# A graph layer's inner node stages: row sums in the add, squares on ScalarE, two tiles ahead

## The chip, the cores and the metric

The kernel runs on one core of one Trainium2 chip. The metric is the device time of one execution in microseconds; a median over several runs is given, lower is better. Five engines work side by side, each through a queue of its own: TensorE (PE in the profile, its weight loads PEld), VectorE (DVE), ScalarE (ACT), GpSimd (POOL) and Sync (SP), which here only issues transfers. They meet through semaphores that the program writes out by hand.

## The reference, cut to what matters

`x` has 6250 rows of 256. Three graph attention layers run over 200,000 edges, beside an attention mixer and, at the end, eight experts. Between two graph layers each node's row is put together, normalised and projected for the next layer:

```python
def _layernorm(x, g, b):
    mu = x.mean(-1, keepdims=True)
    var = ((x - mu) ** 2).mean(-1, keepdims=True)
    return (x - mu) / jnp.sqrt(var + LN_EPS) * g + b
...
h = x
for i, (W, a_s, a_d, b, g, be, heads, concat) in enumerate(layers):
    h_new = _layernorm(_gat_conv(h, src, dst, W, a_s, a_d, b, heads, concat), g, be)
    if i > 0:
        h_new = h_new + h
    h = jax.nn.relu(h_new)
```

Inside `_gat_conv` a node's result is the sum over its incoming edges, one of which is the node itself, each weighted by a softmax. The kernel adds the node's own edge in the stage that follows the edges.

## The kernel before, in words

The program is a row of phases with a barrier after each: `prepare_walk`, then `node_phase` of layer 0, then for each layer `edge_phase` and, after the first two, `node_phase` of the next layer; then `final_phase` and `experts`. The change is in `node_phase` (L568) and in `over_ring` (L454), which unrolls its loops. Layer 0 is called `first` in the code and does less; the two others (layers 1 and 2) are the inner node stages.

A node stage goes over NB = 49 tiles of 128 rows. Tiles live in rings of four buffers (`TILE_RING`), so buffer `slot` serves tiles slot, slot + 4 and so on. `over_ring` writes out the first four or eight tiles, loops over groups of four, and ends with tile 48. `acc`, with the edges' sums of all 49 tiles, stays in SBUF. Each engine has its own stream of steps:

- Sync (L656 to L686): loads own rows (`rows`, L648) and in layer 2 the residual's old rows (`prev`, L650) into the ring, both on one semaphore per buffer. For each tile b in turn it waits until h of tile b is ready, stores it (L662), issues the loads for tile b + 4, and stores the projected rows of tile b - 2 (L669) when they are ready.
- GpSimd (L709, L704): for each tile, the sums in `acc` times their share of the softmax (`weigh_sum`), then the own rows times theirs into the ring `O` (`weigh_own`). The second waits for the loaded rows and for h of tile b - 4, which frees the buffer. Both count on `owned`.
- VectorE (L748 to L812): `gather_in` waits for the rows and both products, adds them (L760), and takes mean and variance with the statistics operation (L763) and its aggregate (L766). `finish` waits for ScalarE's square root, takes its reciprocal (L776), scales (L786) and shifts (L790) and in layer 2 adds the residual (L799); the last one counts on `h_ready`. A step runs the `gather_in` of the next tile interleaved with the `finish` of this one, operation by operation. Operations of one tile that depend on each other wait for the one ahead by semaphore.
- ScalarE (L851 to L890): a step for tile b takes the root for tile b + 1 (L853), copies tile b's transpose out of PSUM (L867, with the relu), then for tile b - 1 copies the projection's parts out (L878, L879, L880) and clears that tile of `acc` by copying zeros over it (L883).
- TensorE (L904, L913, L914): transposes h of tile b, then projects tile b - 1: four matmuls in two row halves and one for the bias.

Ahead of the tiles VectorE computes all softmax shares at once and ScalarE takes one exponential; then GpSimd may begin.

Of the kernel before, what the change touches and what calls it, by code (L numbers as in the profile page):

```python
# [17 lines left out]
ALU = mybir.AluOpType  # L18
# [435 lines left out]
def over_ring(eng, step, peeled=1):  # L454

    assert NB % TILE_RING == 1
    for i in range(peeled):
        for slot in range(TILE_RING):
            step(i, slot, False)
    with eng.Fori(peeled, NB // TILE_RING) as i:  # L460
        for slot in range(TILE_RING):
            step(i, slot, False)
    step(NB // TILE_RING, 0, True)

# [8 lines left out]
def padded_ring_rows(dram, i, slot):  # L473
    return dram[bass.ds((TILE_RING * i + slot) * P, P), :]
# [93 lines left out]
def node_phase(nc, layer, st, io, dr):  # L568
# [6 lines left out]
    first = layer == 0  # L575
    acc, AD, own, terms = st["acc"], st["AD"], st["own"], st["terms"]
    with Phase(nc, f"node{layer}") as ph:
# [6 lines left out]
        stats = ph.sb("stats", [P, TILE_RING, 6])  # L584
# [7 lines left out]
        zeros = ph.sb("zeros", [P, GW])  # L592
# [14 lines left out]
        loaded = [ph.sem(f"loaded{k}") for k in range(TILE_RING)]  # L607
        chain1 = ph.sem("chain1")
# [26 lines left out]
        loads = 1 + (layer >= 2)  # L635
# [9 lines left out]
        def _(sp):  # L645
            def load(i, slot, last):
                if not first:
                    sp.dma_start(rows[:, slot, :], padded_ring_rows(dr["rows"], i, slot)).then_inc(loaded[slot], 16)  # L648
                if layer >= 2:
                    sp.dma_start(prev[:, slot, :], padded_ring_rows(dr["h"], i, slot)).then_inc(loaded[slot], 16)  # L650

            load(0, 0, False)
            load(0, 1, False)
            if not first:
                for n, name in enumerate(("ln_g", "ln_b")):
                    sp.dma_start(vecs[:, n, :], broadcast_row(io[f"{name}{layer - 1}"])).then_inc(vecs_in, 16)  # L656
            for slot in (2, 3):
                load(0, slot, False)
# [12 lines left out]
            for b in range(NB):  # L671
                store_h(b)
                if b + TILE_RING < NB:
                    load((b + TILE_RING) // TILE_RING, b % TILE_RING, b + TILE_RING == NB - 1)
                if b >= 2:
                    store_rows(b - 2)
            for b in (NB - 2, NB - 1):
                store_rows(b)
            for slot in range(TILE_RING):
                n = NB // TILE_RING + (slot == 0)  # L680
                sp.wait_ge(h_out[slot], 16 * n)
                sp.wait_ge(ext_out[slot], 16 * n)
                if first:
                    sp.wait_ge(hT_out[slot], 16 * n)

        @block.gpsimd  # L686
        def _(g):
            g.memset(eps[:, :], LN_EPS).then_inc(consts, 1)
            g.memset(ones3[:, :], 1.0).then_inc(consts, 1)
            if not first:  # L690
                g.memset(zeros[:, :], 0.0).then_inc(consts, 1)
# [6 lines left out]
            def weigh_own(b):  # L698
                slot = b % TILE_RING
                g.wait_ge(loaded[slot], 16 * loads * (b // TILE_RING + 1))  # L700
                if b >= TILE_RING:

                    g.wait_ge(h_ready, b - TILE_RING + 2)
                g.tensor_tensor(by_head(O[:, slot, :]), head_view(rows[:, slot, :]),  # L704
                                es[:, 0, b, :].unsqueeze(2).broadcast_to([P, H, D]), ALU.mult).then_inc(owned, 1)
# [12 lines left out]
        def _(v):  # L718
# [26 lines left out]
            N1 = 1 if first else 2  # L745
            N2 = 1 if first else 2 + (layer >= 2)

            def gather_in(i, slot, last):  # L748

                b = TILE_RING * i + slot  # L750
                ch = Chain(v, chain1, b * N1)
                if first:
                    o = acc[:, bass.ds(b, 1), 0:C].rearrange("p a c -> p (a c)")
                else:
                    v.wait_ge(loaded[slot], 16 * loads * (i + 1))
# [4 lines left out]
                    ch.add(v.tensor_tensor(oh, oh, a, ALU.add))  # L760
                    yield
                    ch.wait()
                ch.add(v.bn_stats(stats[:, slot, :], o))  # L763
                yield
                wait_apart(v, chain1, ch.base + ch.n, passed)
                v.bn_aggr(mv[:, slot, :], stats[:, slot, :]).then_inc(stats_ready, 1)  # L766
                assert ch.n == N1

            def finish(i, slot, last):
# [15 lines left out]
                else:  # L785
# [8 lines left out]
                    else:  # L794
# [3 lines left out]

                        v.scalar_tensor_tensor(out=hn, in0=prev[:, slot, :], scalar=0.0, in1=o, op0=ALU.max, op1=ALU.add  # L799
# [3 lines left out]
            for _ in gather_in(0, 0, False):  # L803
                pass

            def step(i, slot, last):

                following = iter(()) if last else gather_in(i + (slot + 1) // TILE_RING, (slot + 1) % TILE_RING, False)
                for _ in zip_longest(following, finish(i, slot, last)):
                    pass  # L810

            over_ring(v, step)  # L812
# [17 lines left out]
        def _(a):  # L830
# [20 lines left out]
            def std(slot, b):  # L851
                a.wait_ge(stats_ready, b + 1)
                a.activation(sd[:, slot, :], mv[:, slot, 1:2], ACT.Sqrt, bias=eps[:, :]).then_inc(sd_ready, 1)  # L853

            std(0, 0)

            def step(i, slot, last):

                b = TILE_RING * i + slot
                if not last:  # L860
                    std((slot + 1) % TILE_RING, b + 1)
# [10 lines left out]
            def extend(i, slot):  # L872
# [8 lines left out]
                if not first:  # L881

                    a.activation(acc[:, bass.ds(b, 1), :].rearrange("p a c -> p (a c)"), zeros[:, :], ACT.Copy).then_inc(acc_clear, 1)  # L883

            over_ring(a, step, peeled=2)
# [4 lines left out]
            if not first:  # L890
                a.wait_ge(acc_clear, NB)
# [1922 lines left out]
```

## Time and profile before

| | |
|---|---|
| median of 3 runs | 7522.47 us (7515.94 to 7524.8) |
| profiled execution, its own time | 7531.31 us |
| its span in the profile | 7529.6 us |
| VectorE busy | 5498.7 us, 73% |
| TensorE busy | 5390.2 us, 72%, mean granted clock 0.779 |
| GpSimd busy | 5176.0 us, 69% |
| ScalarE busy | 2138.7 us, 28% |
| transfers | 949.93 MB, mean 126 GB/s |

The shares are of the whole span, most of which are the three edge phases; for a stage one has to look at its own stretch. The two inner node stages lie at about 2301 to 2432 us and 4557 to 4712 us. Busy time counts an instruction from its start to its end, also while it waits inside for a port or for its predecessor. The granted clock is a share of TensorE's 2.4 GHz. "Waits" lists put an engine's idle time down to what ended it.

### The profile page before, as it was taken

How to read it: one execution, taken by the hardware profiler on the slowest of the kernel's cores; microseconds unless marked ns; L12 is line 12 of the kernel's file. 1: busy time of each engine (PE TensorE's matmuls, PEld its weight loads, DVE VectorE, ACT ScalarE, POOL GpSimd, SP SyncE). 2: the span in 40 equal slices, each digit the busy share in tenths (PEclk: the TensorE clock that was granted, in tenths of full speed). 3: DMA queues.
4: the chain of work that ended last, by engine and by line, in shares of the span. 5: the costliest groups of instructions: out<-in, count | busy, mean ns of one | idle time of the engine just before them, and what ended most of it. 6: DMA issues, size and time to landing. Idle time of an engine off the chain costs nothing. (4 is left out here: it accounts for less than half of the span.)

```text
span 7529.6 us, 113108 instructions
## 1 busy us (share of the span) xinstructions
PE 5390.2 (72%) x23828; PEld 3495.0 (46%) x23829; DVE 5498.7 (73%) x16160; ACT 2138.7 (28%) x5415; POOL 5176.0 (69%) x5471
## 2 busy tenths in 40 slices
PE   5677777766775677777766666587777876673399
PEld 3344444444443345444544444355555544342398
DVE  6677777777777677777777778677787777778643
ACT  2112121211113233333321113234343421113466
POOL 1777777777774777777777773777777777772444
PEclk8777787877778777777777777678888877776599
DMA  6445455544443444444444444444444444444444
GB/s 211 138 141 145 141 146 141 144 135 140 136 134 116 117 121 123 121 123 122 122 114 111 111 110 139 115 123 128 126 128 125 127 118 111 111 111 139 146 70 64
DMA packets 531615, 949.93 MB, mean 126 GB/s; under 512 B 117850, under 2 KB 366049, under 8 KB 531030
## 3 DMA queue, kind: packets, MB, share of 16 engines
q0 software_dynamic: 259808, 691.84, 34.5%
q1 hardware_dynamic: 254610, 235.89, 10.2%
q10 hardware_dynamic: 16612, 15.96, 0.6%
q8 instruction: 177, 2.90, 0.2%
q14 instruction: 408, 3.34, 0.1%
HBM read 796.92 MB, written 151.73 MB: 126 GB/s over the span
## 5 line engine op out<-in xcount | busy, mean ns | idle before, releaser
L1250 POOL DMA_INDIRECT edges_G<-rows,edges_index x4980 | 4749.4, 954 | 1554.4 <-issue 1481.0
L1450 PE MATMUL edges_ps_o<-edges_G,edges_OH 128*128 128x264 f32 x9960 | 3507.1, 490 | 307.1 <-DVE edges_G L1726 173.9
L1450 PEld LDWEIGHTS edges_ps_o<-edges_G,edges_OH 128*128 128x128 f32 x9960 | 2119.1, 234 | 1127.4 <-issue 634.9
L1744 DVE TENSOR_TENSOR acc<-acc,edges_ps_o 128x264 f32 x2490 | 1048.8, 421 | 821.7 <-PE edges_ps_o L1450 547.6
L1726 DVE TENSOR_TENSOR edges_G<-edges_G,edges_ps_c 128x1024 f32<-128x1024 f32 x1245 | 1500.3, 1205 | 1.8 <-ACT edges_G L1270 1.3
L1294 ACT ACTIVATE edges_OHT<-edges_ps_far 128x512 bf16<-128x512 f32 x1245 | 742.5, 596 | 1331.2 <-PE edges_ps_far L1410 1330.8
L1418 PE MATMUL edges_ps_s<-ident,edges_alpha 128*128 128x128 f32 x249 | 114.4, 459 | 1266.5 <-DVE edges_alpha L1620 1266.5
L1718 DVE TENSOR_TENSOR edges_OH<-edges_ps_c,relT 128x512 f32<-128x512 f32 x1245 | 848.6, 682 | 0.1
L1602 DVE COPY edges_node<-terms 128x12 bf16 x2490 | 476.1, 198 | 292.1 <-issue 73.8
L1418 PEld LDWEIGHTS edges_ps_s<-ident,edges_alpha 128*128 128x128 f32 x249 | 44.2, 177 | 1375.3 <-DVE edges_alpha L1620 1375.3
L1410 PE MATMUL edges_ps_far<-edges_rels,pole_rows 5*128 5x512 bf16 x1245 | 608.4, 489 | 41.3 <-DMA WT<-in_L_mix_b 19.8
L1269 ACT ACTIVATE edges_ps_c<-edges_diff 128x80 f32<-128x80 f32 x249 | 60.0, 241 | 1467.6 <-DVE edges_diff L1706 1467.5
L1410 PEld LDWEIGHTS edges_ps_far<-edges_rels,pole_rows 5*128 5x128 bf16 x1245 | 117.2, 94 | 685.3 <-issue 511.5
L1615 DVE TENSOR_TENSOR edges_tu<-edges_ad,edges_G 128x80 f32<-128x80 f32 x249 | 75.0, 301 | 427.9 <-DMA edges_G<-rows,edges_index 427.0
L2581 POOL DMA_INDIRECT out<-experts_Y,experts_token x105 | 165.2, 1573 | 249.7 <-DMA out<-experts_Y,experts_token 210.6
L1293 ACT ACTIVATE edges_front<-edges_ps_far 128x1 f32<-128x1 f32 x249 | 42.7, 171 | 848.7 <-PE edges_ps_far L1410 848.7
L1280 ACT ACTIVATE edges_fade<-edges_ps_s,edges_front 128x4 f32<-128x4 f32 x249 | 65.7, 264 | 758.7 <-PE edges_ps_s L1437 758.7
L2158 POOL DMA_INDIRECT xslot<-final_XH,final_slots x98 | 101.5, 1036 | 167.7 <-DVE final_slots L2338 139.7
L2607 PEld LDWEIGHTS experts_psH<-experts_xs,experts_Wup 128*128 128x128 f32 x1680 | 206.1, 194 | 5.3
L2607 PE MATMUL experts_psH<-experts_xs,experts_Wup 128*128 128x128 f32 x1680 | 206.4, 277 | 0.0
L2616 PE MATMUL experts_psY<-W,experts_hT 128*128 x840 | 198.6, 379 | 0.2 <-ACT experts_hT L2666 0.2
L913 PE MATMUL node_psB<-Wx,node_hT 128*128 128x264 f32 x588 | 185.4, 445 | 0.0
(377 smaller groups left out, 6211.3 us busy)
## 6 DMA issues: line engine op xcount, KB each, us to landing
edges_G<-rows,edges_index POOLq DMA_INDIRECT x4980
xslot<-edges_blank SPq DMA_DIRECT2D x80, 650.0 KB
edges_masks<-lanes_of SPq DMA_DIRECT2D x123, 192.0 KB
rows<-node_ext SPq DMA_DIRECT2D x147, 130.0 KB, 2.2
experts_X<-xslot SPq DMA_DIRECT2D x105, 130.0 KB, 2.1
node_rows<-rows SPq DMA_DIRECT2D x98, 130.0 KB
h<-node_Hn SPq DMA_DIRECT2D x98, 128.0 KB, 1.7
W<-in_L_ffn_W SPq DMA_DIRECT2D x16, 512.0 KB
```

What stands on the lines that cost most here:

```text
L913: pe.matmul(psB[slot % 2][:, 0:RW + H], hT[:, slot % TILE_RING, k, :], Wx[:, k, :], start=(k == 0), stop=False)
L1250: g.indirect_dma_start(G[n][:, s, 0:RW], None, dr["rows"], bass.IndirectOffsetOnAxis(index[n][:, s:s + 1], 0)).then_inc(gathered[n], 16)
L1294: a.activation(OHT[:, 4 * k:4 * k + 4, :].rearrange("p s e -> p (s e)"), ps_far[:, :], ACT.Relu, bias=1.0, scale=-1.0).then_inc(oht_ready, 1)
L1410: pe.matmul(ps_far[:, :], pole[r, :], rels[r, 4 * k * P:4 * (k + 1) * P], start=True, stop=True).then_inc(far_ready, 1)
L1450: mm = pe.matmul(ps_o[BANK_OF[g]][:, 0:GW], OH[:, 2 * g + j, :], G[n][:, 2 * g + j, :], start=(j == 0), stop=(j == 1))
L1602: ins = v.tensor_copy(node[n][:, g, :], terms[:, bass.ds(b, 1), :, :].rearrange("p a h k -> p (a h k)"))
L1718: v.tensor_tensor(OH[:, 4 * k:4 * k + 4, :], ps_iota.unsqueeze(1).broadcast_to([P, 4, P]), rel.unsqueeze(2).broadcast_to([P, 4, P]), ALU.i ...
L1726: v.tensor_tensor(g4[:, :, :, 0:D], g4[:, :, :, 0:D], ps_w[:, 4 * k:4 * k + 4, :].unsqueeze(3).broadcast_to([P, 4, H, D]), ALU.mult).then_ ...
L1744: v.tensor_tensor(a, a, ps_o[BANK_OF[g]][:, 0:GW], ALU.add).then_inc(added, 1)
L2581: g.indirect_dma_start(out, bass.IndirectOffsetOnAxis(token[:, slot, :], 0), Y[:, slot, :], None, bounds_check=N - 1, oob_is_err=False, co ...
L2607: mm = pe.matmul(psH[slot % 2][:, c * P:(c + 1) * P], Wup[:, slot % 2, k, c * P:(c + 1) * P], xs[:, slot % 2, k, :], start=(k == 0), stop= ...
L2616: mm = pe.matmul(psY[slot % 2][:, 0:C], hT[:, slot % 2, c * P:(c + 1) * P], W2[:, bass.ds(e, 1), c, :].rearrange("p a o -> p (a o)"), star ...
```

## The change

In the two inner node stages:

- VectorE's add becomes a scalar-tensor-tensor operation (times 1.0, plus) that also writes the row's sum into `total`; the statistics operation and its aggregate go. It is issued two tiles ahead instead of one, and at the start of a step, not interleaved.
- ScalarE turns the sum into the mean, squares the centred row with the operation's own summing (into the variance's place), waits for both, and takes the root with the scale that belongs to it. It does so two tiles ahead.
- ScalarE no longer clears `acc`. Sync does, with a transfer from a fourfold zero tile for four tiles at a time, once their rows are summed.
- Sync loads own rows for tile b + 6 as soon as the products of tile b + 2 are done, ahead of the result's store; the residual's old rows have a semaphore of their own, and only the operation that adds them waits for it.
- `over_ring` takes a number of groups to write out at its end, so that the last step's look-ahead can be left out.

The diff, cut to its core:

```diff
-def over_ring(eng, step, peeled=1):
+def over_ring(eng, step, peeled=1, behind=0):
...
-    with eng.Fori(peeled, NB // TILE_RING) as i:
+    with eng.Fori(peeled, NB // TILE_RING - behind) as i:
+        for slot in range(TILE_RING):
+            step(i, slot, False)
+    for i in range(NB // TILE_RING - behind, NB // TILE_RING):
         for slot in range(TILE_RING):
             step(i, slot, False)
     step(NB // TILE_RING, 0, True)
+
+def within(i, slot, ahead):
+    return not isinstance(i, int) or TILE_RING * i + slot + ahead < NB
...
+    LOOK = 1 if first else 2
...
+            def clear(b, n):
+                sp.wait_ge(stats_ready, b + n)
+                sp.dma_start(acc[:, b:b + n, :], zeros[:, 0:n, :]).then_inc(acc_clear, 16)
...
-            for slot in (2, 3):
-                load(0, slot, False)
+                for b in (2, 3):
+                    load_rows(b)
+                if layer >= 2:
+                    for b in range(TILE_RING):
+                        load_prev(b)
+                for b in range(2):
+                    sp.wait_ge(owned, 2 * b + 2)
+                    load_rows(b + TILE_RING)
+                sp.wait_ge(consts, 3)
...
             for b in range(NB):
                 store_h(b)
-                if b + TILE_RING < NB:
-                    load((b + TILE_RING) // TILE_RING, b % TILE_RING, b + TILE_RING == NB - 1)
+                if not first and b + TILE_RING + 2 < NB:
+                    sp.wait_ge(owned, 2 * (b + 2) + 2)
+                    load_rows(b + TILE_RING + 2)
+                if layer >= 2 and b + TILE_RING < NB:
+                    load_prev(b + TILE_RING)
                 if b >= 2:
                     store_rows(b - 2)
+                if not first and b % TILE_RING == 1:
+                    clear(b - 1, TILE_RING)
+            if not first:
+                clear(NB - 1, 1)
             for b in (NB - 2, NB - 1):
                 store_rows(b)
+            if not first:
+                sp.wait_ge(acc_clear, 16 * (NB // TILE_RING + 1))
...
-                g.memset(zeros[:, :], 0.0).then_inc(consts, 1)
+                g.memset(zeros[:, :, :], 0.0).then_inc(consts, 1)
...
-                    v.wait_ge(loaded[slot], 16 * loads * (i + 1))
...
-                    ch.add(v.tensor_tensor(oh, oh, a, ALU.add))
-                    yield
-                    ch.wait()
-                ch.add(v.bn_stats(stats[:, slot, :], o))
+                    v.scalar_tensor_tensor(out=oh, in0=oh, scalar=1.0, in1=a, op0=ALU.mult, op1=ALU.add,
+                                           accum_out=total[:, slot, :]).then_inc(stats_ready, 1)
+                    return
...
+                        v.wait_ge(prev_in[slot], 16 * (i + 1))
                         v.scalar_tensor_tensor(out=hn, in0=prev[:, slot, :], scalar=0.0, in1=o, op0=ALU.max, op1=ALU.add
...
-                following = iter(()) if last else gather_in(i + (slot + 1) // TILE_RING, (slot + 1) % TILE_RING, False)
-                for _ in zip_longest(following, finish(i, slot, last)):
+                ahead = gather_in(i + (slot + LOOK) // TILE_RING, (slot + LOOK) % TILE_RING, False)
+                for _ in zip_longest(ahead if within(i, slot, LOOK) else iter(()), finish(i, slot, last)):
...
+                a.activation(mv[:, slot, 0:1], total[:, slot, :], ACT.Identity, scale=1.0 / C).then_inc(squared, 1)
+                a.activation(square[:, :], O[:, slot, :], ACT.Square, bias=total[:, slot, :], scale=-float(C),
+                             accum_out=mv[:, slot, 1:2]).then_inc(squared, 1)
+                a.wait_ge(squared, 2 * b + 2)
+                a.activation(sd[:, slot, :], mv[:, slot, 1:2], ACT.Sqrt, bias=eps[:, :], scale=1.0 / C ** 3).then_inc(sd_ready, 1)
...
-                if not last:
-                    std((slot + 1) % TILE_RING, b + 1)
+                if within(i, slot, LOOK):
+                    std((slot + LOOK) % TILE_RING, b + LOOK)
...
-                    a.activation(acc[:, bass.ds(b, 1), :].rearrange("p a c -> p (a c)"), zeros[:, :], ACT.Copy).then_inc(acc_clear, 1)
```

## Rows read from the trace of the kernel before

**Rows 1.** List by tile, node_Hn: count, duration ns min/median/max, first and last start
```profile
L790 DVE SCALAR_TENSOR_TENSOR node_Hn<-node_O,node_rstd,node_vecs x49: 483/485/719, 2312.6 to 2426.1; 128x256 f32<-128x256 f32 x49
L799 DVE SCALAR_TENSOR_TENSOR node_Hn<-node_prev,node_O x49: 424/424/803, 4568.7 to 4705.7; 128x256 f32<-128x256 f32 x49
```

**Rows 2.** Table by stretch: PE, PEld, DVE, ACT, POOL us (count), clock, DMA, GB/s
```profile
2313.00:2427.00 114.00, 80.51 (x334) 49.11 (x335) 97.85 (x286) 65.20 (x284) 60.14 (x92) 0.92 0.52 162
4569.00:4706.00 137.00, 104.52 (x330) 62.93 (x330) 114.75 (x334) 64.46 (x279) 60.59 (x91) 0.70 0.57 178
```

**Rows 3.** List of waits, first inner stage: us in total, times, longest us
```profile
POOL node_O L704 <- DMA node_rows<-rows: 48.6, 44, 2.8
...
ACT AD L878 <- PE node_psB L914: 42.9, 49, 1.9
...
DVE node_rstd L776 <- ACT node_sd L853: 13.3, 30, 1.7
...
DVE node_O L760 <- POOL node_O L704: 1.5, 1, 1.5
```

**Rows 4.** List by tile, node_O, columns as in rows 1
```profile
L704 POOL TENSOR_TENSOR node_O<-node_rows,node_es x98: 607/614/884, 2309.0 to 4698.8; 128x256 f32<-128x256 f32 x98
L760 DVE TENSOR_TENSOR node_O<-node_O,acc x98: 410/420/872, 2309.7 to 4701.6; 128x256 f32<-128x256 f32 x98
L763 DVE BATCH_NORM_STATS2 node_stats<-node_O x98: 408/427/430, 2310.5 to 4702.1; 128x6 f32<-128x256 f32 x98
L786 DVE SCALAR_TENSOR_TENSOR node_O<-node_O,node_mv,node_vecs x98: 467/470/907, 2312.1 to 4704.6; 128x256 f32<-128x256 f32 x98
```

**Rows 5.** Order of time, first inner stage, VectorE and GpSimd: start us, us, instruction
```profile
2340.97 0.47 DVE L786 SCALAR_TENSOR_TENSOR node_O<-node_O,node_mv,node_vecs 128x256 f32<-128x256 f32 x1
2341.03 0.88 POOL L709 TENSOR_TENSOR acc<-acc,node_es 128x256 f32<-128x256 f32 x1
...
2341.48 0.72 DVE L790 SCALAR_TENSOR_TENSOR node_Hn<-node_O,node_rstd,node_vecs 128x256 f32<-128x256 f32 x1
...
2343.18 0.91 DVE L786 SCALAR_TENSOR_TENSOR node_O<-node_O,node_mv,node_vecs 128x256 f32<-128x256 f32 x1
2343.19 0.61 POOL L709 TENSOR_TENSOR acc<-acc,node_es 128x256 f32<-128x256 f32 x1
```

**Rows 6.** Order of time near that stage's end, VectorE, no product beside it
```profile
2422.08 0.48 DVE L790 SCALAR_TENSOR_TENSOR node_Hn<-node_O,node_rstd,node_vecs 128x256 f32<-128x256 f32 x1
...
2422.48 0.42 DVE L760 TENSOR_TENSOR node_O<-node_O,acc 128x256 f32<-128x256 f32 x1
...
2425.36 0.17 DVE L776 RECIPROCAL node_rstd<-node_sd 128x1 f32<-128x1 f32 x1 [0.63 <-ACT node_sd L853]
2425.57 0.48 DVE L786 SCALAR_TENSOR_TENSOR node_O<-node_O,node_mv,node_vecs 128x256 f32<-128x256 f32 x1
...
2426.09 0.48 DVE L790 SCALAR_TENSOR_TENSOR node_Hn<-node_O,node_rstd,node_vecs 128x256 f32<-128x256 f32 x1
```

**Rows 7.** Groups of instructions by form, first inner stage, ScalarE: busy us, mean ns
```profile
L867 ACT ACTIVATE node_hT<-node_psA 128x256 f32<-128x256 f32 x49 | 18.8, 384 | 6.4 <-PE node_psA L904 5.4
...
L853 ACT ACTIVATE node_sd<-node_mv,node_eps 128x1 f32<-128x1 f32 x49 | 14.5, 295 | 6.8 <-DVE node_mv L766 6.8
...
L878 ACT ACTIVATE AD<-node_psB 128x4 f32 x40 | 6.9, 174 | 34.4 <-PE node_psB L914 34.4
...
L883 ACT ACTIVATE acc<-node_zeros 128x264 f32 x40 | 17.0, 425 | 0.0
...
L853 ACT ACT_TABLE_LOAD x1 | 1.3, 1283 | 0.0
```

**Rows 8.** List by line, L2425 of a later stage, ScalarE, columns as in rows 1
```profile
L2425 ACT ACTIVATE final_XH<-final_Hn,final_shift,final_scale x49: 583/585/599, 6867.9 to 7076.5; 128x256 f32<-128x256 f32 x49
```

**Rows 9.** List by tile, node_rows and node_prev, Sync's issues, columns as in rows 1
```profile
L648 SPq DMA_DIRECT2D node_rows<-rows x98: 319/433/461, 2301.6 to 4696.1; - x98
...
L650 SPq DMA_DIRECT2D node_prev<-h x49: 422/457/570, 4557.3 to 4696.6; - x49
```

## What the change will do: the prediction, made blind

> **What bounds the kernel now.** Only the two inner node stages change, so I looked for their stretches first and asked what each tile costs there. The list by tile gives the starts of the operation that finishes a tile: 49 of them from 2312.6 to 2426.1 us in the first inner stage and from 4568.7 to 4705.7 us in the second [rows 1]. Divided by 48 that is 2.364 and 2.854 us per tile, 250 us of 7529.6 in all; nothing else in the program can change much.
>
> Then the table by stretch [rows 2]: VectorE is busy 97.85 of 114 us and 114.75 of 137; the next, TensorE, 80.51 and 104.52; GpSimd and ScalarE about half. The list of waits [rows 3] says the rest: VectorE waits 13.3 us for ScalarE's square root in the first stage and only 1.5 us, once, for GpSimd, although GpSimd itself waits 48.6 us for its own rows to land. So late rows cost nothing yet; VectorE's queue sets the pace.
>
> Last, why VectorE's operations take what they take [rows 4]: those with two tensor inputs reach from 410 to 872 and from 467 to 907 ns, while the statistics (one input) stay within 408 to 430. The order of time shows the reason [rows 5]. The scaling that began at 2343.18, 0.01 us ahead of a GpSimd product, ended 0.29 us after that product. A product that began 0.06 us after a scaling (2341.03 against 2340.97) ended 0.47 us after it, and the next VectorE operation 0.29 us after the product. So the two engines take turns, for 0.29 us of each VectorE operation and 0.47 us of each product; the first 0.12 to 0.19 us of a VectorE operation and 0.14 of a product (0.61 - 0.47) lie beside anything.
>
> **The change, part by part.** *VectorE* loses the statistics (0.427 us) and the aggregate behind them in both stages, and the add becomes one that also sums. No row has such an operation. Nearest is the scaling, also two tensors: 0.470 against 0.420 for the plain add [rows 4]. Bounds: 0.42, and 0.93 (twice the streaming, 0.29 more, and a readout as long as the 0.17 us small reciprocal [rows 6]). I take 0.47, the nearest row.
>
> The Trainium skill, Vector Engine (DVE) Microarchitecture Reference, section 7, says that the scalar-tensor-tensor form with two non-bf16 SBUF sources runs at half throughput, for want of a port to read the accumulator back. The scaling is of that form with two fp32 sources and is not half as fast; no row has the accumulating form, which is the rule's case. By the rule the sum is that of the second rival below.
>
> The new chain, undisturbed spacings from [rows 6]: reciprocal to scaling 0.21, scaling to shift 0.52 (each waits for the one ahead), shift to the next tile's first operation 0.40, that is 0.08 ahead of the shift's end. Laid out with the turns, 0 being the end of a tile's last operation: the sum starts at -0.08, takes its turn 0.10 to 0.39. Weighing the own rows of a later tile, which waits for just that end to get its buffer, takes the next turn, 0.39 to 0.86. Reciprocal at 0.31, scaling at 0.52; it wants its turn at 0.71, gets 0.86 to 1.15. The other product waits until then: 1.15 to 1.62. Shift at 1.19, turn 1.62 to 1.91. So **1.91 us a tile** in the first stage. In the second the residual add follows 0.04 us later, 0.42 long [rows 1], with GpSimd waiting for its end: **2.37**. Without a collision it would be 1.52 and 1.98.
>
> *ScalarE* loses the clear (0.425) and gains a small scaling, a square of 256 with a sum, and a wait for both ahead of the root. Bounds from [rows 7]: the small one 0.174 to 0.295; the square between the clear's 0.425 (264 wide) and 0.585 (256 wide, with two per-partition operands [rows 8]), I take 0.50, as it has one; the readout of the sum nothing to 0.295, I take 0.17. With root 0.295, the two wide copies 0.384 each and the two narrow 0.174 each: 2.26, less five joints where operations overlap by about 0.1 (the clear's 0.425 spans more than its place), plus 0.04 for the wait: **1.80** (1.55 to 2.13). Under 1.91, but close. Its waits for the projection (42.9 us, 0.88 a tile [rows 3]) then cover root work. Will the root be late? Behind the end of tile b-1 come TensorE's 1.67 us (below) and 0.55 of narrow and wide copies, some 0.3 after the end of b; squares and root take 1.0; VectorE wants root b+2 at 1.91 + 0.3: 0.9 to spare. So the 13.3 us wait goes; next in line to be late is ScalarE's whole turn (rival 1).
>
> *TensorE* needs 80.51/114 x 2.364 = 1.67 us a tile at granted clock 0.92 (mostly the 2.4 GHz level) and 104.52/137 x 2.854 = 2.18 at 0.70 (a mixture with the 1.2 GHz level) [rows 2]. If the first stage runs some 9 of its tiles as the second ran, 2.18 instead of 1.91, that costs 2.4 us, which I take (bounds nothing and 13 us, for all 48); in the second it stays under the pace.
>
> *Sync's queue* (every issue counts): at most some 0.46 us an issue [rows 9]; three and a quarter a tile are 1.5, four and a quarter 1.95, under the pace. Its new wait for weighed rows b+2 has behind it that load, the result's store and the clear; VectorE needs those rows before it can end tile b, so it passes at once; so does the wait for the sums. Rows for tile b+6 leave at most 0.9 us after the end of b and are wanted two tiles later, 3.8 us; should they come late, GpSimd slips, and VectorE has one more tile of lead. Cost nothing; without that cover each late row costs its lateness.
>
> *Transfers*: busy share 0.52 x 2.364 = 1.23 us a tile for three, 1.63 for four [rows 2], so 0.41 each. A clear of 132 KB per tile at that price: 1.64 of 1.91 and 2.04 of 2.37, 86%. Nothing, as long as it stays under 1. GpSimd's fourfold zeros (0.9 us more) lie in its wait ahead of the shares. The last clear is issued ahead of the last two stores, so it ends nothing.
>
> *Ends*: one tile more is summed and squared before the first is finished, about 1 us a stage.
>
> **Sum**: (2.364 - 1.91) x 48 = 21.8; (2.854 - 2.37) x 48 = 23.2; less 2.4, less 2: 40.6 us. Against the profiled execution, 7531.3, that is 7490.7; that execution lies 8.8 us above the median of the runs, 7522.5, so the median goes to **7482**.
>
> **Rivals.**
> 1. *ScalarE becomes the bound.* For: 1.80 against 1.91, and two of its operations have no row. At its upper prices 2.13: gain (2.364 - 2.13) x 48 + 23.2 - 4.4 = 30, 7492. If a quarter of its 0.88 us wait is uncovered as well, 2.35: almost only the second stage gains, 19.5, 7503. Against: all its other operations overlap today.
> 2. *The summing add takes the upper price, 0.93.* Same layout: turn to 0.68, product to 1.15, scaling to 1.46, product to 1.93, shift to 2.22; 2.68 in the second stage. Gain 6.9 + 8.4 - 4.4 = 11, 7511, which is no change that can be told. Against: the scaling at 0.470.
> 3. *Slower: the turns are held for whole operations.* Then a tile costs the sum of VectorE's two-input operations and both products: 0.47 + 0.47 + 0.485 + 2 x 0.614 = 2.65, 3.08 with the residual. That is (0.29 + 0.22) x 48 = 24 us more than now, 7547. It decides in the first stage once held time exceeds 2.364. For: the products now find no one-input operation to lie beside. Against: today's sum, 0.42 + 0.47 + 0.485 + 1.23 = 2.60, already exceeds the 2.364 that a tile takes. The Trainium skill, SBUF — State Buffer, Who interferes with whom, states this rule: an exclusive lock for the whole instruction, the loser fully blocked. The trace agrees that one waits for the other, and disagrees on the length.
> 4. *The change doesn't do what it says*: square and root don't share ScalarE's loaded table, and each tile loads twice. A load is 1.283 us [rows 7]; 1.80 + 2.57 = 4.37 a tile, (2.01 + 1.52) x 48 = 169 us more, 7691. For: no row has a square. Against: today's copies and root run behind one load per stage. The Trainium skill, ScalarE: Activation LUTs, Table sets, puts cheap functions into every set and doesn't list square among its examples.
>
> **Chances.** Forecast 0.63 (its own range 7463 to 7500; below lies the layout without collisions but ScalarE-bound, some 65 us), ScalarE 0.17, dear sum 0.11, whole-operation turns 0.05, tables 0.04. A measurement here can tell 0.2%, 15 us, so 7507. Faster: 0.63 + 0.15 + 0.02 = 0.80; same 0.02 + 0.08 = 0.10; slower 0.10. The range 7463 to 7512 holds the forecast nearly whole, the first rival and half of the second: 0.8.
>
> **What would show it.** Starts of the finishing operation 1.9 and 2.4 us apart; VectorE's summing add near 0.47 without a collision, products near 0.8 for having to wait; no wait for the root; one table load a stage; transfers' share near 0.85. Spacing of 2.1 or more with VectorE waiting for ScalarE means rival 1; a summing add above 0.7, rival 2; VectorE operations that end 0.4 us and more behind a product, rival 3. The prediction is wrong in its base if transfers land so late that VectorE waits for GpSimd.

## The result and the profile after

The change makes the kernel faster: 7475.84 us (median of 4, 7471.14 to 7477.6) against 7521.8 (median of 4, 7515.94 to 7524.8), ratio 0.9938, 95% interval 0.9922 to 0.9954, 46 us. Forecast were 7482 and a range of 7463 to 7512. The profiled execution took 7475.3 us, its span is 7473.6.

The list by tile of the changed kernel, the lines that answer to [rows 1]:

```profile
L819 DVE SCALAR_TENSOR_TENSOR node_Hn<-node_O,node_rstd,node_vecs x49: 483/717/927, 2309.0 to 2400.9; 128x256 f32<-128x256 f32 x49
L829 DVE SCALAR_TENSOR_TENSOR node_Hn<-node_prev,node_O x49: 424/425/718, 4540.2 to 4652.0; 128x256 f32<-128x256 f32 x49
```

(2400.9 - 2309.0) / 48 is 1.915 us a tile, (4652.0 - 4540.2) / 48 is 2.329. Times 48 the two stages gain 21.6 and 25.2 us, 46.8 together; the layout had 1.91 and 2.37, 45.0. From the first load of rows to the first finished tile the first stage takes 12.2 us instead of 11.0, the forecast microsecond for one more tile summed ahead. (The two profiled spans differ by 56 us; some 9 of it lie outside these stages, as the profiled execution of before was that far above its median.)

The table by stretch, columns as in [rows 2]:

```profile
2309.50:2400.90 91.40, 75.18 (x328) 46.02 (x329) 82.98 (x236) 77.65 (x371) 63.40 (x89) 0.95 0.85 266
4540.70:4652.00 111.30, 80.54 (x330) 49.36 (x330) 102.46 (x284) 78.79 (x370) 65.01 (x89) 0.91 0.91 273
```

The share of the transfers is 0.85 and 0.91 (0.52 and 0.57 before), TensorE's granted clock 0.95 and 0.91: in the second stage it now runs mostly at the 2.4 GHz level, where it was a mixture before (0.70). The order of time of one tile, VectorE and GpSimd:

```profile
2352.57 0.72 DVE L819 SCALAR_TENSOR_TENSOR node_Hn<-node_O,node_rstd,node_vecs 128x256 f32<-128x256 f32 x1
...
2353.20 0.41 DVE L790 SCALAR_TENSOR_TENSOR node_O<-node_O,acc 128x256 f32<-128x256 f32 x1
...
2353.43 0.67 POOL L737 TENSOR_TENSOR node_O<-node_rows,node_es 128x256 f32<-128x256 f32 x1 [0.42 <-DVE node_Hn L819]
...
2353.55 0.08 DVE L790 DVE_READ_ACCUMULATOR node_O<-node_O,acc 128x1 f32 x1
2353.55 0.15 DVE L805 RECIPROCAL node_rstd<-node_sd 128x1 f32<-128x1 f32 x1
...
2353.74 0.63 DVE L815 SCALAR_TENSOR_TENSOR node_O<-node_O,node_mv,node_vecs 128x256 f32<-128x256 f32 x1
...
2354.05 0.79 POOL L742 TENSOR_TENSOR acc<-acc,node_es 128x256 f32<-128x256 f32 x1
...
2354.41 0.72 DVE L819 SCALAR_TENSOR_TENSOR node_Hn<-node_O,node_rstd,node_vecs 128x256 f32<-128x256 f32 x1
...
2355.15 0.42 DVE L790 SCALAR_TENSOR_TENSOR node_O<-node_O,acc 128x256 f32<-128x256 f32 x1
```

This is the order of the forecast layout. About the end of the last shift (2353.29) the sum runs first, the product of own rows waits and ends at 2354.10, the scaling 0.27 after it, the second product waits for the scaling, 0.79 instead of 0.61, and the shift waits for that product, 0.72 instead of 0.48. From shift to shift this tile takes 1.84 us (2354.41 - 2352.57), and that is the steady tile: 24 of the first stage's 48 spacings are 1.83 to 1.90. In the second stage 30 of 48 are 2.29 to 2.31, while every fourth is about 2.62, where VectorE's loop over groups of four starts anew (why was not looked into). Three finishing operations there:

```profile
4611.65 0.43 DVE L829 SCALAR_TENSOR_TENSOR node_Hn<-node_prev,node_O 128x256 f32<-128x256 f32 x1
...
4613.95 0.43 DVE L829 SCALAR_TENSOR_TENSOR node_Hn<-node_prev,node_O 128x256 f32<-128x256 f32 x1
...
4616.57 0.43 DVE L829 SCALAR_TENSOR_TENSOR node_Hn<-node_prev,node_O 128x256 f32<-128x256 f32 x1
```

The layout's 1.91 and 2.37 are therefore 0.07 above the tile that they describe, and meet the means of 1.915 and 2.329 only because longer tiles, for which the layout has no term, are averaged in. The list by tile, answering to [rows 4], and the list of waits in the first stage, answering to [rows 3]:

```profile
L737 POOL TENSOR_TENSOR node_O<-node_rows,node_es x98: 607/663/907, 2304.1 to 4645.4; 128x256 f32<-128x256 f32 x98
L790 DVE SCALAR_TENSOR_TENSOR node_O<-node_O,acc x98: 410/418/829, 2304.9 to 4647.2; 128x256 f32<-128x256 f32 x98
L790 DVE DVE_READ_ACCUMULATOR node_O<-node_O,acc x98: 75/81/84, 2305.5 to 4647.6; 128x1 f32 x98
L889 ACT ACTIVATE node_square<-node_O,node_total x98: 491/507/526, 2305.7 to 4649.4; 128x256 f32<-128x256 f32 x98
L889 ACT ACTIVATION_READ_ACCUMULATOR node_square<-node_O,node_total x98: 185/198/218, 2306.1 to 4649.8; 128x1 f32 x98
L815 DVE SCALAR_TENSOR_TENSOR node_O<-node_O,node_mv,node_vecs x98: 483/633/859, 2308.4 to 4650.9; 128x256 f32<-128x256 f32 x98
```

```profile
POOL node_O L737 <- DVE node_Hn L819: 13.7, 28, 1.2
POOL node_O L737 <- DMA node_rows<-rows: 9.8, 15, 1.9
...
DVE node_rstd L805 <- ACT node_sd L892: 2.1, 4, 0.8
...
DVE node_O L790 <- POOL node_O L737: 0.6, 1, 0.6
```

The summing add has a median of 418 ns and a readout of 81 ns as an instruction of its own; the square is 507 and its readout 198. The wait for the root is 2.1 us where it was 13.3, and GpSimd now waits for freed buffers more than for rows.

### The profile page after: what moved, and what is told of

It reads as the page before. It is cut to its first block and busy times, and to the rows that moved or that the text cites. A ratio compares the mean times of both kernels' runs of the same rounds, so it can differ in the third digit from the quotient of the medians.

```text
span 7473.6 us, 113007 instructions
## 1 busy us (share of the span) xinstructions
PE 5382.7 (72%) x23828; PEld 3486.5 (47%) x23829; DVE 5479.1 (73%) x16062; ACT 2166.4 (29%) x5611; POOL 5173.5 (69%) x5471
## 5 line engine op out<-in xcount | busy, mean ns | idle before, releaser
L1435 PEld LDWEIGHTS edges_ps_s<-edges_node,edges_OHT 128*128 128x128 bf16 x4980 | 161.3, 96 | 45.3 <-ACT edges_OHT L1329 7.2
```

Source lines behind the costliest of these rows:

```text
L1435: mm = pe.matmul(ps_ad[:, s * KEPT:(s + 1) * KEPT], OHT[:, s, :], node[n][:, s // 2, :], start=True, stop=True)
```

## The experiments

The first account was the prediction's: VectorE's chain, shortened by the statistics, and its turns with GpSimd set the pace. Rivals: the transfers set it; the distance is the gain and the sums aren't. Each row has the spacing per tile in both stages, worked out as above from the one profiled execution, and the ratio to the kernel before. "Sums" names the engine that takes mean and variance, "ahead" the tiles of look-ahead; "early" means that the load for tile b + 6 stands behind the store of tile b in Sync's queue, where the load for b + 4 stood ("late"). The residual's own semaphore is in all rows but the first.

| kernel | sums | ahead | rows | clear | 1st | 2nd | ratio (95%) |
|---|---|---|---|---|---|---|---|
| before | VectorE | 1 | late | ScalarE | 2.364 | 2.854 | 1 |
| after | ScalarE | 2 | early | transfer | 1.915 | 2.329 | 0.9938 (0.9922 to 0.9954) |
| e1_clear_scalar | ScalarE | 2 | early | ScalarE | 1.896 | 2.327 | 0.9937 (0.9921 to 0.9954) |
| e2_one_ahead | ScalarE | 1 | early | transfer | 2.477 | 2.819 | 1.0011 (1.0002 to 1.0021) |
| e3_late_rows | ScalarE | 2 | late | transfer | 2.794 | 3.065 | 1.0044 (1.0027 to 1.0061) |
| e4_statistics | VectorE | 2 | early | transfer | 1.904 | 2.410 | 0.9945 (0.9928 to 0.9961) |
| e7_sums_alone | ScalarE | 1 | late | ScalarE | 2.881 | 3.379 | 1.0053 (1.0038 to 1.0069) |
| e8_ahead_and_rows | VectorE | 2 | early | ScalarE | 1.902 | 2.415 | 0.9944 (0.9931 to 0.9958) |
| e10_rows_alone | VectorE | 1 | early | ScalarE | 2.290 | 2.802 | 0.9990 (0.9981 to 0.9999) |
| e11_ahead_alone | VectorE | 2 | late | ScalarE | 2.842 | 3.100 | 1.0055 (1.0040 to 1.0071) |

**One part undone at a time.** First the clear, back on ScalarE:

```diff
+                if not first:
+                    a.activation(acc[:, bass.ds(b, 1), :].rearrange("p a c -> p (a c)"), zeros[:, 0, :], ACT.Copy).then_inc(acc_clear, 1)
...
-                if not first and b % TILE_RING == 1:
-                    clear(b - 1, TILE_RING)
```

> The changed kernel, but the clearing of acc goes back from transfers to ScalarE. Theory (VectorE's chain and its turns with GpSimd set the pace, 1.915 and 2.329 us a tile; ScalarE stands behind it at about 1.76): ScalarE rises by 0.31 to about 2.07, so the first inner stage goes to about 2.07 and the second stays near 2.33; some 7 us more than the changed kernel, about 7483. Rival (the transfers, busy for 0.86 and 0.90 of the stages, set the pace): the share falls by a quarter and both stages get shorter, under 1.9 and 2.3, or stay.

Its table by stretch, first and second inner stage:

```profile
2307.00:2397.50 90.50, 82.70 (x328) 46.26 (x329) 82.20 (x236) 85.98 (x416) 64.11 (x89) 0.97 0.66 200
4536.50:4647.70 111.20, 83.06 (x330) 50.53 (x330) 101.90 (x283) 91.52 (x416) 64.68 (x89) 0.89 0.71 215
```

The theory's 2.07 did not come, nor the rival's shorter stages. The transfers' share fell to 0.66 and 0.71 and the pace stayed, so in the changed kernel transfers don't set it; and ScalarE had room for the clear: busy 85.98 / 90.5 x 1.896 = 1.80 us a tile with it, 1.63 without. Moving the clear was worth nothing.

Then the distance, one tile instead of two:

```diff
-    LOOK = 1 if first else 2
+    LOOK = 1
```

> The changed kernel with sums and roots one tile ahead instead of two. Theory: ScalarE takes root b+1 only after the copies of tile b-2 (some 2.4 us after the end of tile b-1), 1.0 more for mean, squares and root, and then VectorE needs 1.25 to 1.6 to the end of tile b+1; so two tiles take 4.7 to 5.0, 2.35 to 2.5 a tile in the first stage and about 0.25 more in the second, with VectorE waiting for ScalarE's root: 7515 to 7525, the gain gone. Rival (VectorE's shorter queue is the gain, the distance is of no account): 1.9 and 2.35 as before, 7476.

In its list of waits of the first stage:

```profile
DVE node_rstd L805 <- ACT node_sd L892: 37.1, 46, 2.1
```

As the theory had it (2.477; the second stage a little above): VectorE waits 37.1 us for the root, as ScalarE has the squares to do ahead of it (with the statistics on VectorE the wait is 13.8, e10 below), and the whole gain is gone.

Then the rows, loaded after the tile's end as before:

```diff
-                for b in range(2):
-                    sp.wait_ge(owned, 2 * b + 2)
-                    load_rows(b + TILE_RING)
...
-                if not first and b + TILE_RING + 2 < NB:
-                    sp.wait_ge(owned, 2 * (b + 2) + 2)
-                    load_rows(b + TILE_RING + 2)
+                if not first and b + TILE_RING < NB:
+                    load_rows(b + TILE_RING)
```

> The changed kernel, but own rows are loaded as in the kernel before: those of tile b+4 behind the store of tile b. Theory: they land about 2.4 us after the end of tile b (issue 0.75, landing), the product takes 0.65, and the sum of b+4 is due already at the start of step b+2, so two tiles take 2.4 + 0.65 + 1.95 = 5.0, 2.5 a tile, and 2.7 in the second stage; VectorE waits for GpSimd and GpSimd for the rows: about 7520. Rival (late rows still cost nothing, as in the kernel before): unchanged, 7476.

In its list of waits of the first stage:

```profile
POOL node_O L733 <- DMA node_rows<-rows: 71.3, 44, 3.3
...
DVE node_O L786 <- POOL node_O L733: 40.9, 23, 2.3
```

GpSimd waits 71.3 us for rows, and now VectorE waits 40.9 us for GpSimd, where in [rows 3] it was 1.5. The direction is the theory's, the size was 0.3 to 0.4 us a tile short. So that late rows cost nothing held for the kernel before, with its sums one tile ahead, and no longer for two.

Last the sums and squares, on VectorE's statistics again:

```diff
-                    v.scalar_tensor_tensor(out=oh, in0=oh, scalar=1.0, in1=a, op0=ALU.mult, op1=ALU.add,
-                                           accum_out=total[:, slot, :]).then_inc(stats_ready, 1)
...
+                    v.tensor_tensor(oh, oh, a, ALU.add).then_inc(chain1, 1)
...
                 v.bn_stats(stats[:, slot, :], o).then_inc(chain1, 1)
...
-                a.activation(square[:, :], O[:, slot, :], ACT.Square, bias=total[:, slot, :], scale=-float(C),
-                             accum_out=mv[:, slot, 1:2]).then_inc(squared, 1)
...
```

> The changed kernel, but VectorE takes the statistics again (plain add, statistics, aggregate) and ScalarE only the root; two tiles ahead, early rows and clears by transfer stay. Theory: VectorE's undisturbed tile was 2.16 in the kernel before and turns added 0.2: 2.3 in the first stage, 2.7 in the second, no wait for the root; about 10 us under the kernel before, 7512. Rival (the distance and the early rows are the gain, the sums a small part): near 2.0 and 2.4, about 7482.

Here the theory fell and the rival held. With the statistics back the first stage is as fast in the mean as without them (1.904 against 1.915) and the second loses 0.08 x 48 = 4 us of 25. The steady tile does lose: 1.93 and 2.39 against 1.84 and 2.30. In the first stage the changed kernel gives that back in longer tiles, seven of them 2.2 to 2.6 us, where e4 has one. The 2.16 that I had called undisturbed contained a wait for the root: the tile of the kernel before that runs from the shift at 2422.08 [rows 6] to the one at 2424.25 is 2.17 us long and has 0.40 of it. In the second stage that wait came to 18.0 us. The line of that tile, and the one of the second stage's list of waits, both before:

```profile
2423.30 0.16 DVE L776 RECIPROCAL node_rstd<-node_sd 128x1 f32<-128x1 f32 x1 [0.40 <-ACT node_sd L853]
```

```profile
DVE node_rstd L776 <- ACT node_sd L853: 18.0, 20, 1.5
```

**Parts alone.** So I built the parts by themselves, from the edits above. First those of e1, e2 and e3 together, which leaves only the sums and squares of the change (and the residual's own semaphore):

> The summing add and the squares on ScalarE alone: one tile ahead, own rows loaded behind the store of tile b for b+4, clears on ScalarE. Theory: ScalarE's step grows by the squares and keeps the clear, and the root is wanted one tile later only: the end of ScalarE's step at 2.7 us after a tile's end, 1.0 for the root, 1.6 for VectorE's rest, 5.3 for two tiles: 2.65 in the first stage and 2.9 in the second, slower than the kernel before (2.364, 2.854): about 7540. Rival (VectorE's 0.4 us less a tile is worth its own): 2.0 and 2.45, about 7485.

From its list of waits, first stage up to 2440 us (it ends at 2447):

```profile
DVE node_rstd L795 <- ACT node_sd L882: 46.8, 31, 3.1
```

Slower than before by more than forecast, 44 us instead of 20 (7563.67 against 7519.72): with the sums one tile ahead the root is waited for 46.8 us, where it was 13.3 [rows 3]. Alone, what the title names first costs time.

The next three have the statistics back (e4's edit) and the clear on ScalarE (e1's). With no more than that it is the distance and the rows together; with e2's as well it is the rows alone, with e3's the distance alone:

> Of the change only two parts: two tiles ahead, and own rows loaded as places come free. Statistics stay on VectorE and clears on ScalarE. Theory after the first runs (the gain comes from these two together, which end the wait for the root; fewer operations on VectorE are a small part): 1.90 us a tile in the first stage and 2.41 in the second, as with the statistics put back into the changed kernel; about 0.9945 of the kernel before. Rival (the prediction's own account, that VectorE's lost operations are the gain): 2.3 and 2.7, 0.998.

> Of the change only the early rows: one tile ahead, statistics on VectorE, clears on ScalarE. Theory: GpSimd's waits for rows go, but VectorE did not wait for GpSimd, so the pace stays at 2.36 and 2.85, with the wait for the root as it was: within 5 us of the kernel before. Rival (early rows are the gain): 2.0 and 2.5, about 0.995.

> Of the change only the distance: two tiles ahead, rows loaded behind the store of tile b for b+4, statistics on VectorE, clears on ScalarE. Theory: the sum of tile b+4 is due at the start of step b+2 while its rows land 2.4 us after the end of b and take 0.65 to be weighed: two tiles take some 5.2 us, 2.6 in the first stage and 2.85 in the second, with VectorE waiting for GpSimd: slower by about 10 us than the kernel before. Rival (the distance alone is the gain): 1.95 and 2.4, about 0.995.

The first of these three is the change without its sums, squares and clears, and it has nine tenths of the gain (0.9944 against 0.9938, which the intervals do not tell apart); its theory held. The waits of the other two, rows alone and distance alone, first stage:

```profile
DVE node_rstd L800 <- ACT node_sd L879: 13.8, 26, 1.6
```

```profile
POOL node_O L727 <- DMA node_rows<-rows: 73.6, 44, 4.6
...
DVE node_O L781 <- POOL node_O L727: 34.4, 23, 3.3
```

Rows alone leave the wait for the root (13.8 us); the distance alone turns late rows into VectorE's wait (34.4 us). Alone, the rows gain 6 us, hardly clear of the noise, and the distance loses 41, where 10 were forecast; together they gain 41. (The runs with late rows, e3, e7 and e11, all came out slower than forecast; why is left open.) Why the statistics cost so little there, the table by stretch and one tile of e8 in order of time show:

```profile
2312.60:2403.40 90.80, 73.74 (x326) 45.18 (x327) 90.66 (x283) 60.10 (x276) 66.89 (x89) 0.96 0.67 197
4543.80:4659.20 115.40, 88.74 (x328) 54.37 (x329) 111.42 (x329) 63.35 (x277) 68.77 (x89) 0.82 0.69 208
```

```profile
2351.74 0.41 DVE L785 TENSOR_TENSOR node_O<-node_O,acc 128x256 f32<-128x256 f32 x1
...
2351.96 0.67 POOL L731 TENSOR_TENSOR node_O<-node_rows,node_es 128x256 f32<-128x256 f32 x1 [0.43 <-DVE node_Hn L814]
...
2352.08 0.15 DVE L800 RECIPROCAL node_rstd<-node_sd 128x1 f32<-128x1 f32 x1
...
2352.19 0.43 DVE L788 BATCH_NORM_STATS2 node_stats<-node_O 128x6 f32<-128x256 f32 x1
...
2352.53 0.47 DVE L810 SCALAR_TENSOR_TENSOR node_O<-node_O,node_mv,node_vecs 128x256 f32<-128x256 f32 x1
...
2352.59 0.88 POOL L736 TENSOR_TENSOR acc<-acc,node_es 128x256 f32<-128x256 f32 x1
...
2353.04 0.71 DVE L814 SCALAR_TENSOR_TENSOR node_Hn<-node_O,node_rstd,node_vecs 128x256 f32<-128x256 f32 x1
...
2353.68 0.41 DVE L785 TENSOR_TENSOR node_O<-node_O,acc 128x256 f32<-128x256 f32 x1
```

VectorE is busy for 90.66 of 90.8 us in the first stage and for 111.42 of 115.4 in the second, where it was idle for 16 of 114 us and 22 of 137 before [rows 2]. So some 34 of the 43 us that the two stages gain are idle time that went, 31 of them the wait for the root (13.3 and 18.0); the rest is time inside its operations, which are the same as before but collide less. While the product of own rows holds its turn (2351.96 to 2352.63) VectorE does the reciprocal and the statistics, which take no turn; the scaling at 2352.53 finds the turn free. In the changed kernel the scaling comes some 0.25 us earlier and waits for that same product. Most of the statistics filled a wait; taking them and the aggregate away (0.43 and 0.17 us) left the wait and gained 0.09 us of the steady tile (1.93 to 1.84).

**The turns and what lies beneath.** Two runs took turns away. The first leaves out one of GpSimd's two products:

```diff
-                    weigh_sum(b)
...
-                    v.wait_ge(owned, 2 * b + 2)
+                    v.wait_ge(owned, b + 1)
```

> The changed kernel without the weighing of the edges' sums: GpSimd makes one product a tile, the sums are added unweighed (that part of the computation is left out). Theory (turns): the shift no longer waits for a second product; laid out, 1.67 in the first stage, where ScalarE then sets about 1.76, and 2.13 in the second: 15 to 18 us under the changed kernel, about 7459. Rival (transfers set the pace): both stages unchanged, 1.915 and 2.33. Rival (ScalarE sets the pace of the first stage already): first unchanged, second faster.

1.827 and 2.279, ratio 0.9920 (0.9905 to 0.9935): faster, by less than the layout says. The first tiles of each stage do follow the layout (1.61 and 2.07 us, laid out 1.67 and 2.13), but GpSimd now waits 44.1 us for rows in the first stage (9.8 in the changed kernel). The second keeps all the work and moves the two constant rows of VectorE's scaling and shift into PSUM:

```diff
+                c0.link(v.tensor_copy(psV[:, 0:2 * C], vecs[:, :, :].rearrange("p k c -> p (k c)")))
...
-                    ... scalar=mv[:, slot, 0:1], in1=vecs[:, 0, :],
+                    ... scalar=mv[:, slot, 0:1], in1=psV[:, 0:C],
-                    ... scalar=rstd[:, slot, :], in1=vecs[:, 1, :],
+                    ... scalar=rstd[:, slot, :], in1=psV[:, C:2 * C],
```

> The changed kernel with the two rows of the normalisation (gain and shift) copied once per stage into PSUM and read from there: scaling and shift then have one SBUF input each. All of the computation stays. Theory (turns are taken by operations with two SBUF inputs): scaling and shift no longer wait for products nor hold them up; they may each take some 0.05 longer for the PSUM read. First stage about 1.76 (ScalarE), second about 2.10: 15 to 18 us under the changed kernel, about 7459. Rival (any VectorE operation with two tensors takes turns, or transfers set the pace): unchanged or 5 us slower.

Its lists by tile, the scaling (both stages) and the first stage's shift; its first two shifts in order of time; its table by stretch; and from its list of waits, second stage:

```profile
L817 DVE SCALAR_TENSOR_TENSOR node_O<-node_O,node_mv,node_psV x98: 479/481/483, 2307.0 to 4643.2; 128x256 f32<-128x256 f32 x98
L821 DVE SCALAR_TENSOR_TENSOR node_Hn<-node_O,node_rstd,node_psV x49: 480/481/481, 2307.5 to 2396.3; 128x256 f32<-128x256 f32 x49
```

```profile
2307.53 0.48 DVE L821 SCALAR_TENSOR_TENSOR node_Hn<-node_O,node_rstd,node_psV 128x256 f32<-128x256 f32 x1
...
2308.98 0.48 DVE L821 SCALAR_TENSOR_TENSOR node_Hn<-node_O,node_rstd,node_psV 128x256 f32<-128x256 f32 x1
```

```profile
2308.00:2396.30 88.30, 74.86 (x328) 46.34 (x329) 72.31 (x237) 75.49 (x372) 53.50 (x89) 0.95 0.88 275
4534.60:4644.30 109.70, 83.82 (x330) 51.06 (x330) 99.64 (x284) 78.22 (x370) 56.44 (x89) 0.87 0.90 275
```

```profile
POOL node_O L738 <- DMA node_rows<-rows: 42.3, 34, 2.6
```

The scaling is never lengthened now (479 to 483 ns, 98 times, against 483 to 859): with one SBUF input it takes no turn. Where the rows are there in time, with both products beside it, the tile falls from 1.84 to 1.45 us (2308.98 - 2307.53), so the turns are what held the changed kernel's steady tile. Yet the stages only reach 1.850 and 2.296, ratio 0.9927 (0.9914 to 0.9941), and in the second GpSimd waits 42.3 us for rows: with the turns shortened, late rows come next, and behind them probably the transfers (share 0.88 and 0.90). So e9 is e6 with the clears' transfers gone as well, and not back on ScalarE but on GpSimd:

```diff
+                    if b >= TILE_RING:
+                        g.memset(acc[:, b - TILE_RING, :], 0.0).then_inc(acc_clear, 1)
```

> The changed kernel with gain and shift read from PSUM (as before) and the clears done by GpSimd, for the tile whose buffer has just been freed, in place of transfers. All of the computation stays. Theory (with the turns shortened the transfers, busy for 0.88 and 0.90, were the next bound at 1.85 and 2.30): without the clears the share falls to about 0.7 and the pace to ScalarE's and TensorE's 1.65 to 1.75 in the first stage and VectorE's 2.1 in the second: 15 us under the run with PSUM alone, about 0.991 of the kernel before. Rival (turns at the summing add and the residual still set the pace, transfers don't): 1.85 and 2.30 stay, 0.9927.

Its lists by tile (the operations that finish a tile), its table by stretch, the wait for rows in the second stage, and the clears in the first:

```profile
L821 DVE SCALAR_TENSOR_TENSOR node_Hn<-node_O,node_rstd,node_psV x49: 480/481/482, 2306.7 to 2388.9; 128x256 f32<-128x256 f32 x49
L831 DVE SCALAR_TENSOR_TENSOR node_Hn<-node_prev,node_O x49: 424/429/758, 4526.9 to 4624.4; 128x256 f32<-128x256 f32 x49
```

```profile
2307.20:2388.90 81.70, 77.79 (x328) 46.49 (x329) 71.36 (x236) 75.08 (x372) 69.51 (x138) 0.96 0.76 220
4527.40:4624.40 97.00, 74.11 (x330) 45.44 (x330) 88.50 (x283) 78.37 (x370) 67.46 (x138) 0.97 0.87 247
```

```profile
POOL node_O L732 <- DMA node_rows<-rows: 15.5, 25, 1.0
```

```profile
L745 POOL MEMSET acc<- x45: 311/314/318, 2307.9 to 2384.0; 128x264 f32 x45
```

1.713 and 2.031 us a tile, 7450.27 us, ratio 0.9909 (0.9894 to 0.9924): the fastest kernel of the study, 69 us under the one before. The row wait fell to 15.5 us. That it was the clears' transfers and not the shift of GpSimd's work by the clears, no run separates; the shares are 0.76 and 0.87, not the 0.7 forecast, as the tiles are shorter too.

Last, e9 with e4's edit, the statistics on VectorE:

> The fastest kernel so far (gain and shift in PSUM, clears on GpSimd) with the statistics put back on VectorE and only the root left to ScalarE: what the sums and squares are worth once the turns are short. All of the computation stays. Theory (with turns the shift waited about 0.24 us a tile, 0.72 against 0.48, whichever form the sums have): 1.90 - 0.24 = 1.66 to 1.72 in the first stage, where TensorE and the queue's other work keep it, and 2.41 - 0.24 = 2.17 in the second, against 1.71 and 2.03: 5 to 8 us more than the fastest kernel, about 0.9918 of the kernel before. Rival (the sums are worth their 0.4 us of VectorE once it is not held up): 2.1 and 2.45, 0.996.

1.754 and 2.192, 7456.59 us, ratio 0.9917 (0.9904 to 0.9931). The theory held. By the spacings, against 1.713 and 2.031, the sums and squares are worth 2 and 8 us here, more than in the change as made; the two ratios' intervals overlap.

## Why the prediction was right

- *The sum.* 40.6 us were forecast, 46 measured. First stage 21.8 against 21.6, second 23.2 against 25.2; the ends 2 for both stages against 1.2 in the first; the 2.4 us for TensorE's clock did not come (granted 0.95). That the first stage fits to 0.2 us is partly luck: the steady tile is 0.07 us shorter than laid out, and tiles that were not laid out, some with rows that came late, are as much longer.
- *The new chain.* The summing add was taken at 0.47 and is 0.418 with a readout of 0.08, of which nothing shows, as the reciprocal starts beside it. The turns came in the order laid out, each up to 0.07 earlier, mostly because the add was sized 0.05 too long. Rival 3, turns for whole operations, asks 2.65 a tile where 1.915 were measured, and is ruled out.
- *ScalarE.* Square 0.507 (taken 0.50), readout 0.198 (0.17), mean 0.204 (0.174); but its whole turn is 1.63, not 1.80: in the first stage its durations sum to 107.7 us, of which it is busy for 78.1, so 0.6 us a tile overlaps, six joints of 0.1 where five were taken, and the 0.04 for the wait isn't busy time. Rival 1 never came near: with the clear put back as well, 1.80 a tile (e1), the pace stayed. One table load a stage, so rival 4 is out.
- *Transfers.* 0.86 forecast, 0.85 and 0.91 measured, at no cost in the change as made (e1). "Nothing, as long as it stays under 1" was too simple: at 0.88 and 0.90 (e6) GpSimd waits 42.3 us for rows in the second stage, and 15.5 once the clears' transfers are gone (e9).
- *Where the account failed.* "VectorE loses the statistics" stood as the gain's first source; the wait for the root was named as one that goes, and the early rows were costed at nothing. The runs show the reverse: the end of the wait for the root was most of the gain; the second tile ahead ended it, the early rows kept a wait for GpSimd from taking its place (34.4 us in e11), and the statistics lay for the most part beside a product. The layout gave the right time, because it described the kernel after; it was never laid out for the kernel without that part, and so could not tell which part paid. "Late rows cost nothing yet" held, but with the second tile ahead they make the kernel slower than before, by 41 us with the statistics on VectorE (e11) and by 33 without (e3).

## What to carry to other kernels

Lay out the steady tile for the change and also for the change less each of its parts: a part whose time lies beside another engine's turn is worth little until that turn is gone. A part can lose alone and gain beside another: a longer look-ahead ends one wait and needs its inputs earlier, so change both. Compare a layout with the spacings one by one and not only with their mean, which can be right while two misses cancel. Where VectorE and GpSimd take turns, a constant operand that is read from PSUM instead of SBUF took two operations out of the turns, at a price of 0.01 us or less here.

## What the runs showed of the hardware

Reading one of two tensors from PSUM cost VectorE next to nothing (0.481 us for scaling and shift, against 0.470 and 0.485, the medians before) and freed the operations from the turns with GpSimd. The Trainium skill, SBUF — State Buffer, Who interferes with whom, names two SBUF inputs as the condition, and these rows agree; its lock for the whole instruction doesn't agree with 1.84 us for a tile whose five operations with turns would fill 2.65. The Trainium skill, in the same section, says that a GpSimd operation that only writes doesn't contend, and no run here shows that: GpSimd's zeroing took 311 to 318 ns each of 45 times in e9's first stage, but only nine of them overlap one of VectorE's operations with two SBUF inputs, by at most 0.11 us. A summing add on VectorE with two fp32 inputs took 410 ns at its shortest, as the plain add, with a readout of 75 to 84 ns as an instruction of its own; on ScalarE the readout took 185 to 218. The Trainium skill, Vector Engine (DVE) Microarchitecture Reference, section 7, has that form at half throughput; these rows disagree, with a median of 418 ns against 420 for the plain add [rows 4].
